# Two staging buffers in turn for the projected pairs of the second attention, and one store of q moved ahead of a weight load

## The reference

```python
h = layernorm(x) * (1 + ca) + sa            # the modulation comes from c @ wmod
x = x + ga * attn(h)                        # first attention
h = layernorm(x) * (1 + cb) + sb
x = x + gb * ffn(h)                         # rmsnorm, second attention, rmsnorm, 8 experts (top 2)

def attn(x):          # 32 query heads of 64, 8 key/value heads, window of 128, sinks
    q, k, v = split(x @ qkv_w.T + qkv_b)
    q, k = rope(q), rope(k)                 # rotation
    ...
def attention(h, wq, wk, wv, wo):           # inside ffn: same heads, causal, no rotation, no bias
    q, k, v = h @ wq, h @ wk, h @ wv
    ...
```

## Time and profile before

| | |
|---|---|
| three timed runs | 1060.79, 1061.67, 1062.79 us, median 1061.67 |
| span of the profiled execution | 1063.1 us, 22951 instructions |
| mean granted TensorE clock | 0.962 |
| HBM read and written | 105.88 MB and 58.79 MB |
| transfers issued by SP (queue q1) | 143.58 MB, 52.0% of the 16 engines' time |

### The profile page before, as it was taken

The page is one execution under the profiler, slowest core; times in us unless marked ns, Lnnn a source line. Parts: engine busy times, 40 slices in busy tenths (PEclk is TensorE's granted clock), DMA queues, the critical chain, the costliest instruction groups (busy, mean ns, idle before and its releaser), DMA issues.

```text
span 1063.1 us, 22951 instructions
## 1 busy us (share of the span) xinstructions
PE 965.1 (91%) x6862; PEld 901.5 (85%) x6862; DVE 789.4 (74%) x2308; ACT 753.5 (71%) x2122; POOL 466.7 (44%) x550
## 2 busy tenths in 40 slices
PE   5589999999899899999999999999998589999991
PEld 3379899998789799988999999999887489999991
DVE  6779998989899577777777777777764756666646
ACT  3368788887888688788888778877884346555641
POOL 4346668777656333433444332232222852222243
PEclk8899999999999899999999999999997699999996
DMA  8799879787476675465557455354303365555313
GB/s 178 185 233 274 208 190 276 209 213 201 112 177 147 167 190 155 122 164 135 136 140 166 122 168 120 110 153 126 71 1 120 115 221 172 166 170 162 103 58 116
DMA packets 146059, 166.18 MB, mean 156 GB/s; under 512 B 79194, under 2 KB 100714, under 8 KB 140816
## 3 DMA queue, kind: packets, MB, share of 16 engines
q1 hardware_dynamic: 129440, 143.58, 52.0%
q0 software_dynamic: 3712, 11.16, 3.3%
q10 hardware_dynamic: 12784, 9.97, 3.0%
HBM read 105.88 MB, written 58.79 MB: 155 GB/s over the span
## 4 chain that ended last, share of the span: by engine, by line
PE 56%; DVE 17%; issue 10%; ACT 9%; DMA 4%; POOL 1%; SPq 1%; DVEq 0%; ACTq 0%; POOLq 0%
PE psO L1086 14%; PE psS L1053 10%; PE psX L1063 8%; PE psY L1102 6%; PE psP L985 6%; ACT wgt_hi L1319 3%; DVE pbuf L1734 2%; DVE gated L2074 2%; DVE pTl L1756 2%; PE psO L1069 2%; PE psS L1236 2%; PE psP L998 2%; ACT relu_s L1624 2%; PE psX L1236 1%; DVE den L1748 1%
## 5 line engine op out<-in xcount | busy, mean ns | idle before, releaser
L1351 ACT ACTIVATE pbuf<-pbuf,nmax 128x256 f32<-128x256 f32 (+3 forms) x512 | 264.9, 519 | 45.8 <-DVE nmax L1734 44.7
L1053 PE MATMUL psS<-kT,qE 128*128 128x256 f32 (+3 forms) x1024 | 238.2, 317 | 25.7 <-DVE nmax L1734 24.1
L1734 DVE CUSTOM_DVE_ANT_0 pbuf<-psS,mcau 128x256 f32<-128x256 f32 (+3 forms) x512 | 219.9, 435 | 46.9 <-PE psS L1053 41.0
L1756 DVE TENSOR_TENSOR pTl<-psX,pTh 128x512 fp32r<-128x512 f32 x272 | 187.1, 688 | 73.5 <-ACT pTh L1319 72.9
L1319 ACT ACTIVATE pTh<-psX 128x512 fp32r<-128x512 f32 x272 | 160.7, 591 | 55.7 <-PE psO L1086 39.3
L1053 PEld LDWEIGHTS psS<-kT,qE 128*128 128x128 f32 x1024 | 160.2, 192 | 40.3 <-DVE nmax L1734 33.7
L1086 PE MATMUL psO<-pTh,vpad 128*128 128x256 f32 x1088 | 187.1, 294 | 3.2 <-DVE oS L1762 2.0
L798 POOL TENSOR_TENSOR ol<-oS,oh 128x256 fp32r<-128x256 f32 x128 | 94.8, 741 | 200.7 <-ACT oh L1319 196.2
L1063 PE MATMUL psX<-idn,pbuf 128*128 128x128 f32 x1088 | 162.2, 274 | 3.1 <-DVE pTl L1756 3.1
L1086 PEld LDWEIGHTS psO<-pTh,vpad 128*128 128x128 f32 x1088 | 150.3, 190 | 10.5 <-DVE oS L1762 5.4
L1063 PEld LDWEIGHTS psX<-idn,pbuf 128*128 128x128 f32 x1088 | 126.5, 141 | 9.4 <-DVE pTl L1756 3.3
(11 more groups left out here) (295 smaller groups left out, 2369.0 us busy)
## 6 DMA issues: line engine op xcount, KB each, us to landing
qd<-st SPq DMA_DIRECT2D x32, 1024.0 KB, 4.5
qE<-qd SPq DMA_DIRECT2D x128, 256.0 KB, 6.0
mrawV<-in_w_moe SPq DMA_DIRECT2D x32, 384.0 KB
mrawB<-in_w_moe SPq DMA_DIRECT2D x32, 384.0 KB
kT<-kd SPq DMA_DIRECT2D x64, 128.0 KB, 4.4
kT<-kd SPq DMA_DIRECT2D x32, 256.0 KB, 4.3
kd<-st SPq DMA_DIRECT2D x7, 1024.0 KB, 4.8
xg<-sq ACTq DMA_DIRECT2D x7, 640.0 KB, 6.1
```

Source lines behind the costliest of these rows:

```text
L1053: last = mm(psS[j % 2][:, 0:n], qE[:, g % 2, j, t * P:(t + 1) * P], kT[:, g % 2, c, k0:k0 + n], start=(c == 0), stop=(c == 1))
L1351: nc.scalar.activation(pj, pj, ACT.Exp, bias=nmax[:, u % 4, j:j + 1], scale=-1.0, accum_out=sums[:, u % 4, j:j + 1]).then_inc(a_exp, 1)
L1734: V.tensor_tensor_reduce(probs(u, j), psS[j % 2][:, 0:n], mcau[:, SEQ - n:], -SCALE, 3e38, ALU.add, ALU.min, nmax[:, u % 4, j:j + 1]).then ...
L1756: V.tensor_tensor(pTl[:, kt % 2, :], psX[kt % 2][:, :], pTh[:, kt % 2, :], ALU.subtract).then_inc(v_pl, 1)
```

## The change

The pairs of the second attention use two buffers in turn. The second is `tmp`, which the rotation no longer needs once the last rotated pair is through; it has the same size and is viewed in the stage's shape. `SIDE` says which buffer a pair has (0 the stage, 1 `tmp`), `SENT` the value of that side's semaphore after the pair's store; `st_out` becomes a list of two. A copy waits for the pair before on the same side. On side 1 it also waits until POOL has done all of its rotation work (`g_pl`). Besides, in m = 7 of `step_window` the store of q is issued before the load of the output weight instead of behind it.

```diff
@@ -120,7 +120,7 @@
 
 
 
-ITEM, HIGH, PAIR, OUT = {}, {}, {}, []
+ITEM, HIGH, SIDE, SENT = {}, {}, {}, {}
 
 
 def count_items():
@@ -134,12 +134,13 @@
         high += by_scalar(item)
         HIGH[item] = high
         if item[0] in "qk" and item[2] == 1:
-            PAIR[item[:2]] = len(PAIR)
-            OUT.append((OUT[-1] if OUT else 0) + (0 if item[:2] == ("k", 0) else 16))
+            pair = item[:2]
+            SIDE[pair] = (1 + sum(SIDE[p] >= 0 and by_scalar(p + (0,)) for p in SIDE)) % 2 if by_scalar(item) else 0
+            SENT[pair] = 0 if pair == ("k", 0) else 16 * (1 + sum(SIDE[p] == SIDE[pair] and SENT[p] > 0 for p in SENT))
 
 
 count_items()
-WPAIRS = [k for k in PAIR if not by_scalar((k[0], k[1], 0)) and k != ("k", 0)]
+WPAIRS = [k for k in SIDE if not by_scalar((k[0], k[1], 0)) and k != ("k", 0)]
 TURN = {k: n + 1 for n, k in enumerate(WPAIRS)}
 
 
@@ -231,6 +232,11 @@
         oS = sb_att("oS", [P, 2, 2 * P])
         oh = sb_att("oh", [P, 2, 2 * P], F32R)
         ol = sb_att("ol", [P, 2, 2 * P], F32R)
+        sides = [st, tmp[:, :, :].bitcast(F32R).rearrange("p (c r) n -> p c r n", c=2)]
+
+        def stage(pair):
+            return sides[SIDE[pair]]
+
         biasraw = oS[0:33, :, :].rearrange("p c n -> p (c n)")
         wmod_s = pbuf[:, 0:KC * NMOD].rearrange("p (k n) -> p k n", k=KC)
         tmp0 = pbuf[:, KC * NMOD:KC * NMOD + 4 * SEQ].rearrange("p (c n) -> p c n", c=4)
@@ -342,7 +348,7 @@
         ld_wo = sem("ld_wo")
         ld_q = sem("ld_q")
         ld_kt = sem("ld_kt")
-        st_out = sem("st_out_of_stage")
+        st_out = [sem("st_out_of_stage0"), sem("st_out_of_stage1")]
         st_k = sem("st_k0")
         ld_e = [sem(f"ld_e{q}") for q in range(NPC)]
         ld_xg = sem("ld_xg")
@@ -517,11 +523,12 @@
                 else:
                     sp.wait_ge(v_pj, ITEM["q", g, 1])
                 wait(sp, ld_q, 64 * (g - 1))
-                sp.dma_start(qd[g % 2], st[:, :, :, :].bitcast(F32).rearrange("p c r n -> p (c r) n")).then_inc(st_out, 16)
+                sp.dma_start(qd[g % 2], stage(("q", g)).bitcast(F32).rearrange("p c r n -> p (c r) n"))\
+                    .then_inc(st_out[SIDE["q", g]], 16)
 
             def place_q(g):
                 slot = g % 2
-                sp.wait_ge(st_out, OUT[PAIR["q", g]])
+                sp.wait_ge(st_out[SIDE["q", g]], SENT["q", g])
                 wait(sp, ld_q, 64 * g)
                 wait(sp, s_S, 4 * QM * (g - 1))
                 if g == 1:
@@ -547,14 +554,15 @@
                 else:
                     sp.wait_ge(v_pj, ITEM["k", quad, 1])
                 wait(sp, ld_kt, 64 * min(4 * (quad - 1), NG // 2) + 32 * max(4 * (quad - 1) - NG // 2, 0))
-                sp.dma_start(kd[slot], st[:, :, :, :].bitcast(F32).rearrange("p c r n -> p (c r) n")).then_inc(st_out, 16)
+                sp.dma_start(kd[slot], stage(("k", quad)).bitcast(F32).rearrange("p c r n -> p (c r) n"))\
+                    .then_inc(st_out[SIDE["k", quad]], 16)
 
             def place_k(g):
                 quad, i = divmod(g, 4)
                 if quad == 0:
                     sp.wait_ge(st_k, 16)
                 else:
-                    sp.wait_ge(st_out, OUT[PAIR["k", quad]])
+                    sp.wait_ge(st_out[SIDE["k", quad]], SENT["k", quad])
                 wait(sp, ld_kt, 64 * min(g, NG // 2) + 32 * max(g - NG // 2, 0))
                 wait(sp, s_S, 4 * QM * (g - 1))
                 src = kd[quad % 2].rearrange("p (c r) n -> p c r n", c=2)
@@ -635,8 +643,8 @@
                 if m == 6:
                     load_wq(g + 5)
                 if m == 7:
+                    store_q(g + 3)
                     load_wo(g + 2)
-                    store_q(g + 3)
                 if m == 8:
                     place(g + 3)
                 if m == 10:
@@ -1339,9 +1347,12 @@
                     dst = vpad[:, index % 2, 0, part, HD:9 * HD].rearrange("p (g x) -> p g x", x=2 * HD)[:, :, 0:HD]
                     copy(dst, ps[:, 0:4 * HD].rearrange("p (g d) -> p g d", g=4)).then_inc(a_pj, 1)
                 else:
+                    pair = (kind, index)
                     if part == 0:
-                        act.wait_ge(st_out, OUT[PAIR[kind, index] - 1])
-                    copy(st[:, 0, part, :], ps[:, :]).then_inc(a_pj, 1)
+                        wait(act, st_out[SIDE[pair]], SENT[pair] - 16)
+                        if SIDE[pair]:
+                            act.wait_ge(g_pl, 2 * len(WPAIRS))
+                    copy(stage(pair)[:, 0, part, :], ps[:, :]).then_inc(a_pj, 1)
 
             def exp_head(u, j):
                 act.wait_ge(v_max, QM * u + j + 1)
@@ -1452,8 +1463,7 @@
 
             def rope_high(pair):
                 n = TURN[pair]
-                if PAIR[pair] > 0:
-                    act.wait_ge(st_out, OUT[PAIR[pair] - 1])
+                wait(act, st_out[0], SENT[pair] - 16)
                 for r in range(2):
                     act.wait_ge(r_sum, 2 * n - 1 + r)
                     copy(st[:, 0, r, :], tmp[:, 2 * r, :]).then_inc(a_rh, 1)
@@ -1716,7 +1726,8 @@
                               for c in (1, 0))
                     V.tensor_tensor(lo, ps[:, 0:4 * HD].rearrange("p (g d) -> p g d", g=4), hi, ALU.subtract).then_inc(v_pj, 1)
                 else:
-                    V.tensor_tensor(st[:, 1, part, :], ps[:, :], st[:, 0, part, :], ALU.subtract).then_inc(v_pj, 1)
+                    two = stage((kind, index))
+                    V.tensor_tensor(two[:, 1, part, :], ps[:, :], two[:, 0, part, :], ALU.subtract).then_inc(v_pj, 1)
 
             def take(item):
                 if by_scalar(item):
```

## The result

The changed kernel takes 1053.51 us (median of 4 runs, 1051.03 to 1054.91) against 1061.72 us (4 runs, 1060.79 to 1062.79) before. The ratio is 0.9925 with a 95% interval of 0.9906 to 0.9944, so 8 us less, between 5.9 and 10.0. The forecast was 1054.3. One run of the kernel before, timed beside the last experiments, took 4280.14 us; it is left out of the ratios, and nothing here explains it.

The account below looks back on a forecast made before the run. PE was taken as the bound, losing time in one hole near 350 us. Idle 5.03 plus clock 2.55 gave 7.58, taken as 7.4 us, other terms nothing: 1061.67 - 7.4 = 1054.3 us, range 1052.3 to 1057.8.

Parts of the forecast that it names:

- The wait, its place and its one occurrence: ACT's copy of ("k", 4, 0), step 54, waits 5.9 us for the store of ("q", 15), once in the run.
- The idle time, 5.03 us: PE's stop before step 55's third scores goes; PE resumes at 350.38 instead of 355.41 us, gaining 5.03 us.
- The clock, 2.55 us: PE's matmuls after the stop no longer run at clock 0.50: 2.16 + 0.39 = 2.55 us, at the least nothing.
- What is late next: ACT, DVE and transfers must keep up with PE's 7.58 us; DVE slightly behind, so 7.4 us taken; q groups in time.
- the nine added waits: ACT's waits before scalar pairs rise from 20 to 29; between nothing and 0.5 us, taken as nothing.
- The order: At m = 7 the store goes out 1.7 us earlier: worth 1.7 us with the old stage, nothing more with the sides.
- rival D: Slower: output weight stuck behind the store, `high_wo` at m = 9 of four quads, up to 1069.5 us; chance 0.04.
- the serial case: Store served to its end before the weight: first quad's weight lands at 95.0 us, 3.1 early; costs nothing at median landings.
- The total: 7.4 us off the median of 1061.67 gives 1054.3 us; the shift passes unchanged to the end.

Follow-up runs that it names:

- sides alone: Changed kernel with the weight load put back in front of the store of q at m = 7; ratio 0.9912, median 1053.54 us.
- first k pair alone: Changed kernel with only the first k pair of the second attention in `tmp`, the 19 later pairs in the stage; ratio 0.9922, median 1054.1 us.
- the other turn: Changed kernel with the turn started on the other side: first k pair in the stage, next in `tmp`; ratio 0.9986, median 1060.26 us.
- order alone: Kernel before, one stage, with the store of q issued before the output weight load at m = 7; ratio 0.9979, median 1059.88 us.
- second profiles: Kernel before and changed kernel, each run and profiled again: ratio 1.0001, median 1061.18 us, and ratio 0.9925, median 1052.88 us.
- the queue freed: Kernel before with the store before the output weight load and, in the first attention's last quad, four query weight loads behind it; twice: ratios 0.9999, 0.9993.
- mask first: Changed kernel with DVE's modulation of a tile put behind the fourth head's mask in steps 41 to 44; ratio 0.9954, median 1056.12 us.
- store held back: Kernel before with the last q pair's store waiting until PE has done the second scores of step 55; ratio 1.0019, median 1062.34 us.

## Why the prediction was right

*The wait, its place and its one occurrence*: right, and shown by four runs. Without it (sides alone, first k pair alone) the gain is whole; with two buffers but the wait in place (the other turn) the hole is there; with the wait made longer the hole is longer.

*The idle time, 5.03 us*: right. PE goes from the transposes to the scores in 352.35 - 352.21 = 0.14 us; the 0.24 that I gave the slot was 0.1 too much.

*The clock, 2.55 us*: right in kind, a little small. PE's next start moved by 355.41 - 350.28 = 5.13 us, which leaves 7.79 - 5.13 = 2.66. What I had not seen is that this term depends on when the rate comes back: after the 4.58 us of idle in the order alone the same 16 matmuls took 4.16 us, after 4.89 us they took 4.86.

*What is late next*: mis-sized. I held back 0.2 us because DVE would be behind. It was not: it waits 0.49 us for ACT's second copy and ACT 0.44 for PE. PE has the whole 7.7 us. POOL's `tmp` was free in time, groups 14 and 15 came without a wait, and the shift passes: the stretch 54-124 takes 421.08 us before and 420.93 after, and 421.01 and 421.07 in the second profiles, which also prices the nine added waits at nothing that can be seen.

*The order*: nothing with the sides, right. Alone it was priced at 1.7 us as 1.7 us less of waiting. The term failed in its make-up: the wait shrank by 0.3 us and the clock gave the rest of the 1.47 us at PE. The step that failed is that a store issued 1.7 us earlier also lands 1.7 us earlier. Before and with the order alone it lands 6.67 and 6.35 us after POOL's last subtraction (353.61 - 346.94 and 354.58 - 348.23), though it was issued 1.74 and 0.02 us after it. With the same order it lands 5.7 us after it in the other turn and 5.8 and 5.2 in the whole change, so what the order gains at the store is 0.3 to 1.5 us from profile to profile, and in none the 1.7.

*The weight behind the store*, rival D: out. In the first quad of the changed kernel the store's issue alone took 2.64 us and the weight followed at 90.67, 9.6 us before its use; no wait of `woh` on `woraw` is in any profile.

```profile
87.99 2.64 SPq L526 DMA_DIRECT2D qd<-st  x1
90.67 0.43 SPq L517 DMA_DIRECT2D woraw<-in_wo_attn  x1
```

Less the 2.2 us by which this execution started later, that is 1.5 us behind the 86.94 of before, not the 0.45 at most that I had put. In all four quads the weight landed behind the store, by 0.6 to 1.8 us, in the first at 96.6, 3.6 us before its use: the serial case, and nobody waits. The Trainium skill's rule from "DMA: Bandwidth & Descriptors", section "Queues, rings and completion order", made the serial case the one to price. The trace has that order for this weight, but not for every transfer behind a store: with the queue freed the store issued at 348.37 landed 5.17 us later, at 353.54, and the first query weight load, issued at 348.76, landed 3.9 us later, at 352.7, ahead of it. The rule speaks of each DMA engine by itself, and no row here shows which engines a transfer used, so the runs don't isolate it. The median landing of `woraw` is 3.9 us in the changed kernel, 3.6 before.

*The total*: 1054.3 forecast, 1053.51 measured. That it is so near is in part luck. The forecast says that nothing more changes behind the hole. One thing does: the last three steps, 124-127, take 16.95 us after and 18.5 before. Both have the same wait of 2.3 us there, and then PE's clock is another. The wait before and after:

```profile
796.66 0.66 PE L1063 MATMUL psX<-idn,pbuf 128*128 128x128 f32 x4 [2.32 <-DVE pTl L1756]
```

```profile
790.79 0.66 PE L1071 MATMUL psX<-idn,pbuf 128*128 128x128 f32 x4 [2.31 <-DVE pTl L1767]
```

The table by stretch, before and after, over the 8 us from just ahead of that wait's end:

```profile
796.00:804.00 8.00, 7.26 (x46) 6.92 (x47) 4.00 (x9) 3.13 (x7) 1.52 (x3) 0.79 0.00 0
```

```profile
790.00:798.00 8.00, 7.16 (x58) 6.74 (x59) 4.27 (x10) 3.86 (x9) 1.52 (x3) 1.00 0.00 0
```

In six profiles the clock falls at this place (before twice, order alone, other turn, freed queue twice: 18.45 to 18.51 us) and in six it doesn't (whole change twice, sides, first k pair, mask first, store held back: 16.94 to 16.96). The store held back has the longest hole and is among those without, so it isn't the hole as such. It may be a matter of when PE arrives there; no run was made for that, and why is open. With it the change is worth 7.7 + 1.5 = 9.2 us by the profiles, inside the intervals of the timed runs (5.9 to 10.0 for the change) but above the 8.0 in their middle.

Profiles and times agree no better than that in general. Counted from mark 0 to mark 127, the store held back is 0.7 to 1.0 us shorter than before and is timed 2.0 longer; the freed queue is 2.3 to 3.1 shorter and is timed 0.1 and 0.7 shorter; the mask first is 1.0 to 1.3 longer than the whole change and is timed 3.2 longer. The rest of such a difference must lie outside these marks, or in executions that no profile caught; the runs don't say which. The remaining scatter sits in start-up (mark 0 falls between 68.2 and 73.3 us in twelve profiles) and in the experts (249.0 to 255.2).

## What to carry to other kernels

Where one buffer passes from one producer pattern to another, look at the first use after the switch: a wait that was met 37 times out of 38 can cost its whole length the one time the new pattern is a step faster. A second buffer for that single pair was worth as much as taking turns throughout. And when a transfer is late, see what stands ahead of it in the queue before issuing it earlier: issued 2.5, 4.5 and 7.4 us after the loads ahead of it, the same store took 6.3, 4.9 and 3.9 us to land.

## What the runs showed of the hardware

- A short stop of PE costs more than its length, and not in proportion. Over the idle time as the profile counts it, the stretch 52-54 lost 18.18 - 10.39 - 4.89 = 2.9 us before, 18.99 - 10.39 - 5.57 = 3.0 with the store held back, 16.71 - 10.39 - 4.58 = 1.7 with the order alone, 16.03 - 10.39 - 3.96 = 1.7 with the other turn, and 15.58 - 10.39 - 3.40 = 1.8 with the queue freed. Matmuls of 0.63 us instead of 0.40 stand behind every one of these stops, the shortest of which was 3.2 us.
- Behind the stop of 3.40 us the first matmuls still ran at full rate, and the slow ones began 0.7 us after the restart:

```profile
355.33 0.51 PE L1055 MATMUL psS<-kT,qE 128*128 128x256 f32 x2 [3.40 <-DVE nmax L1736]
...
355.80 0.28 PE L1104 MATMUL psY<-woh,ol 128*128 128x256 f32 x1
...
356.03 0.41 PE L1104 MATMUL psY<-woh,oh 128*128 128x256 f32 x1
```

- An idle time of 2.3 us in the last steps was followed by the lower clock in six profiles and not in six others, the same way in both profiles of each of the three kernels that were profiled twice.
- A store of 1 MB landed 5.21 to 6.33 us after its issue when it followed the transfers of q and four weight loads by 2.5 to 3.4 us (six profiles), 4.87 to 4.93 when it followed them by 4.5 to 4.9 (three), and 3.88 when it followed them by 7.4 (one). With the weight loads behind it, it took 5.17 and 4.96.
